# Attention on one Trainium2 core: the reciprocal of a slot's row sum moves behind the next slot's row maximum in VectorE's order

## The chip, the cores and the metric

The kernel runs on one core of a Trainium2 chip. The metric is the device time of one execution in microseconds, given as the median over several runs. A profiled execution gives the trace.

## The reference

Two layers on x of shape 8 x 512 x 256 with a context of the same shape: an mLSTM-like mixing with four heads and a GELU MLP (layer 0), then cross attention with 16 heads and a mixture of eight experts (layer 1). The change lies in the cross attention:

```
q = query @ W_Query + B_Query          # query: layer norm of x, 8 x 512 x 256
k = key @ W_Key + B_Key                # key = value = context
v = value @ W_Value + B_Value
q, k, v -> (B, L, H = 16, D = 64)
scores = einsum('bqhd,bkhd->bhqk', q, k) / D ** 0.5
probs = softmax(scores, axis=-1)
out = einsum('bhqk,bkhd->bqhd', probs, v)
return out.reshape(B, Lq, H * D) @ W_Output + B_Output
```

## The kernel before

`attention` goes through U = 64 units: eight batches times eight pairs of heads. A unit `u` is one pass of the outer loop; its NBL = 8 slots `j` are the two heads times four blocks of 128 query rows. Each engine has the two loops written out for itself, in an order of its own, and the engines meet by semaphores alone. Within its engine an instruction waits for the one in front of it, so the written order is the order of the work. The loop of each engine runs once more than there are units, so that the tail of unit u-1 lies in the first slots of unit u.

The way of a slot through the engines:

- TensorE, `score(u, j)` (L958): scores of 128 rows against 512 keys, two matmuls in float32r, into one of two PSUM banks (`S_BANK + j % 2`). It waits until the exponential of slot j-2 is done.
- VectorE, `row_max(u, j)` (L1153): the negated maximum of each row, into `nmax`. It waits for the scores (`s_ps`).
- ScalarE (L1093): the exponential with the maximum as bias, into `Pr`, with the row sum accumulated into `rsum`. It waits for `nmax` and for the turn of slot j-4.
- VectorE, `row_sum(u, j)` (L1158): the reciprocal of `rsum` into `rinv`. It waits for the exponential (`exp`).
- GpSimd (L1128): `Pr` times `rinv`. It waits for `rinv` and signals `pn`.
- TensorE, `turn(u, j)` (L969): four transposes of `Pr` into one of two banks. It waits for `pn` and for the copy of the turned slot j-2.
- VectorE, `keep(u, j)` (L1165), or ScalarE for slots 4 and 5 (L1112): the turned block into `PT`.

TensorE's order within a unit: in slot j `score(u, j)` and then `turn(u, j-2)` (in slots 0 and 1 it is turn 6 and turn 7 of the unit before). Besides, in slots 0 and 1 it projects the queries and keys of the next unit (`project`, L937), in slot 2 it weighs the values of the unit before (`weigh_values`, L979), in slot 4 it projects the values of the next (`project_values`, L946), in slots 5 and 6 it multiplies by the output weights (`output`, L989). In fourteen units it also turns rows (`turn_rows`, L999) or maps gates (`map_gates`, L1008), in slots 3 and 7.

VectorE's order within slot j: the reciprocal of slot j-1, the maximum of slot j, the copy of turned slot j-2. Besides, it takes part in the next unit's queries (L1140, slot 1) and keys (L1147, slot 2), in the layer norm for the experts in some units, and at slot 7 it takes the reciprocal of slot 7 and adds the outputs of the unit before to x (L1172).

The `% 4` of `Pr`, `nmax`, `rsum` and `rinv` gives each of them four buffers.

Of the kernel before, what the change touches and what calls it, by code (L numbers as in the profile page):

```python
# [826 lines left out]
def attention(nc, c, x_all, xnT_all, ctxT_all, first, Wq, Wk, Wv, Wo, gate_w, lg, rows, rows_in, out, landed):  # L827
# [3 lines left out]
    with ExitStack() as ctx:  # L831
# [33 lines left out]
        def there(u):  # L865
            return 0 <= u < U

        def routed(u, r):

            return u // HP - 1 if u >= HP and u % HP == r else None  # L870
# [16 lines left out]
        with nc.Block() as block:  # L887
# [247 lines left out]
            def _(dve):  # L1135
                def queries(u):
                    dve.wait_ge(s["qh"], u + 1)
                    for h in range(2):
                        own, other = slice(AD * h, AD * h + AD), slice(AD - AD * h, 2 * AD - AD * h)
                        ins = dve.scalar_tensor_tensor(out=q2[other, u % 2, h, :], in0=ps[own, A_BANK, :],  # L1140
                                                       scalar=b_s[own, 0, u % HP:u % HP + 1],
                                                       in1=q2[own, u % 2, h, :], op0=ALU.add, op1=ALU.subtract)
                    ins.then_inc(s["ql"], 1)

                def keys(u):
                    dve.wait_ge(s["kh"], u + 1)
                    dve.scalar_tensor_tensor(out=k_own[:, 1, :], in0=ps[:, A_BANK + 1, :],  # L1147
                                             scalar=b_s[:, 1, u % HP:u % HP + 1],
                                             in1=k_own[:, 0, :], op0=ALU.add, op1=ALU.subtract).then_inc(s["kl"], 1)

                def row_max(u, j):
                    dve.wait_ge(s["s_ps"], NBL * u + j + 1)
                    dve.tensor_reduce(nmax[:, j % 4:j % 4 + 1], ps[:, S_BANK + j % 2, :], AX.X, ALU.max, negate=True  # L1153
                                      ).then_inc(s["nmax"], 1)

                def row_sum(u, j):
                    dve.wait_ge(s["exp"], NBL * u + j + 1)
                    dve.reciprocal(rinv[:, j % 4:j % 4 + 1], rsum[:, j % 4:j % 4 + 1]).then_inc(s["rinv"], 1)  # L1158

                def keep(u, j):  # L1160
                    if j in ON_ACT:
                        return
                    dve.wait_ge(s["t_ps"], NBL * u + j + 1)
                    q = P * (j % TPB)
                    dve.tensor_copy(PT[:, u % 2, j // TPB, :, q:q + P],  # L1165
                                    ps[:, T_BANK + j % 2, :].rearrange("p (t q) -> p t q", t=TPB)).then_inc(s["pt_v"], 1)

                def add_out(u, half):
                    dve.wait_ge(s["y_ps"], 2 * u + half + 1)
                    at = (u // HP) * TPB + 2 * half  # L1170
                    xv = x_all[:, at:at + 2, :].rearrange("p t d -> p (t d)")
                    dve.tensor_tensor(xv, ps[:, Y_BANK - half, :], xv, ALU.add).then_inc(s["x"], 1)  # L1172

                def take_stats(b, t):
                    if t == 0:
                        dve.wait_ge(s["x"], 2 * HP * (b + 1))
                    ins = dve.bn_stats(stats[:, t, :], x_tile(b, t))
                    if t == TPB - 1:
                        ins.then_inc(s["stats"], 1)

                def finish_stats(b):
                    wait_apart(dve, s["stats"], b + 1)
                    for t in range(TPB):
                        ins = dve.bn_aggr(mv[:, t, :], stats[:, t, :])
                    ins.then_inc(s["mv"], 1)
                    dve.wait_ge(s["mv"], b + 1)
                    wait_count(dve, s["rstd"], b)
                    dve.tensor_scalar(ve[:, :], mv[:, :, 1], LN_EPS, None, ALU.add).then_inc(s["ve"], 1)

                def apply(b, t):  # L1190
                    if t == 0:
                        dve.wait_ge(s["rstd"], b + 1)
                    ins = dve.tensor_scalar(xn_tile(b, t), x_tile(b, t), mv[:, t, 0:1], rstd[:, t:t + 1],
                                            ALU.subtract, ALU.mult)
                    if t == TPB - 1:
                        ins.then_inc(s["xn"], 1)
# [11 lines left out]
                for u in range(U + 1):  # L1208
                    for j in range(NBL):
                        if there(u):  # L1210
                            if j >= 1:
                                row_sum(u, j - 1)
                            row_max(u, j)
                            if j >= 2:
                                keep(u, j - 2)
                        if j < 2 and there(u - 1):
                            keep(u - 1, NBL - 2 + j)
                        if there(u + 1):
                            if j == 1:
                                queries(u + 1)  # L1220
                            if j == 2:
                                keys(u + 1)
                        if 2 <= j < 2 + TPB and routed(u, NORM) is not None:
                            take_stats(routed(u, NORM), j - 2)
                        if j == 2 + TPB and routed(u, NORM) is not None:
                            finish_stats(routed(u, NORM))
                        if 2 <= j < 2 + TPB and routed(u, APPLY) is not None:
                            apply(routed(u, APPLY), j - 2)
                        if j == 7:
                            if there(u):  # L1230
                                row_sum(u, j)
                            if there(u - 1):
                                if u > 1:
                                    dve.wait_ge(s["x"], 2 * (u - 1))
                                add_out(u - 1, 0)
                                add_out(u - 1, 1)
# [503 lines left out]
```

## Time and profile before

| what | value |
|---|---|
| time, median of 3 runs | 1844.12 us (1844.11 to 1846.59) |
| the profiled execution's span | 1843.2 us |
| its mean granted TensorE clock | 0.947 |
| TensorE busy | 1663.1 us (90%) |
| VectorE busy | 1209.8 us (66%) |
| ScalarE busy | 843.8 us (46%) |
| GpSimd busy | 608.1 us (33%) |

The span reaches from the first to the last instruction of one profiled execution. The engines' shares are means over stages with different limits: the attention takes the stretch from about 370 to 1640 us, and the router and the experts follow it. TensorE's matmuls are pipelined, and the ends of their records are modelled. A granted clock of 1 is 2.4 GHz.

### The profile page before, as it was taken

To read this page: it belongs to the slowest core of one execution; us is meant where nothing else is said; L and a number is where in the kernel's file an instruction comes from. 1 tells how busy PE (TensorE), PEld (TensorE's weight loads), DVE (VectorE), ACT (ScalarE), POOL (GpSimd) and SP (SyncE) were. 2 spreads that over 40 slices of the span, in tenths; PEclk is the share of its full clock that TensorE was granted. 3 is DMA by queue.
4 is the path that set the end of the run, shared out by engine and by line. 5 is a ranking of instruction groups with operands and counts; after the bars stand their busy time and mean duration, and the time that the engine had idled before them with its cause. 6 is when DMAs were issued, how large, how long until landed. Compare 5 with 4: busy or idle time off the path is not lost. (4 is left out here: it accounts for less than half of the span.)

```text
span 1843.2 us, 25796 instructions
## 1 busy us (share of the span) xinstructions
PE 1663.1 (90%) x8789; PEld 1128.1 (61%) x8789; DVE 1209.8 (66%) x2689; ACT 843.8 (46%) x1870; POOL 608.1 (33%) x730
## 2 busy tenths in 40 slices
PE   6569999996999999999999999999999999973584
PEld 4447777754666666666666666666666766642352
DVE  6445656532777777776776776776777677757761
ACT  3324343431555555555555555555555555531110
POOL 2143445430333323332332332333232323220375
PEclk9669999997999999999999999999999999985697
DMA  8100000003323232323232322222223223213254
GB/s 254 27 23 12 12 12 1 1 0 106 69 47 69 47 92 46 69 69 69 47 92 47 67 72 61 54 65 74 56 60 79 59 53 86 46 45 99 44 85 58
DMA packets 68961, 109.46 MB, mean 59 GB/s; under 512 B 18400, under 2 KB 50400, under 8 KB 68832
## 3 DMA queue, kind: packets, MB, share of 16 engines
q1 hardware_dynamic: 62688, 99.29, 22.1%
q0 software_dynamic: 6144, 8.52, 3.0%
q8 instruction: 72, 1.18, 0.3%
q14 instruction: 57, 0.47, 0.1%
HBM read 27.84 MB, written 12.85 MB: 22 GB/s over the span
## 5 line engine op out<-in xcount | busy, mean ns | idle before, releaser
L1128 POOL TENSOR_SCALAR at_Pr<-at_Pr,at_rinv 128x512 f32<-128x512 f32 x512 | 355.8, 695 | 841.2 <-DVE at_rinv L1158 841.2
L1093 ACT ACTIVATE at_Pr<-at_ps,at_nmax 128x512 f32<-128x512 f32 x512 | 352.2, 688 | 535.2 <-DVE at_nmax L1153 533.6
L1153 DVE TENSOR_REDUCE at_nmax<-at_ps 128x1 f32<-128x512 f32 x512 | 351.2, 686 | 154.0 <-PE at_ps L958 142.5
L958 PE MATMUL at_ps<-at_k,at_q 128*128 128x512 f32 x1024 | 420.7, 492 | 10.8 <-DMA at_k<-at_k_own 9.1
L969 PE MATMUL at_ps<-k_ident,at_Pr 128*128 128x128 f32 x2048 | 309.8, 274 | 4.5 <-POOL at_Pr L1128 4.5
L969 PEld LDWEIGHTS at_ps<-k_ident,at_Pr 128*128 128x128 f32 x2048 | 250.5, 140 | 90.2 <-POOL at_Pr L1128 27.7
L1165 DVE COPY at_PT<-at_ps 128x512 f32<-128x512 f32 x384 | 261.4, 681 | 0.0
L958 PEld LDWEIGHTS at_ps<-at_k,at_q 128*128 128x128 f32 x1024 | 174.6, 191 | 130.7 <-issue 121.2
L979 PE MATMUL at_ps<-at_PT,at_V 128*64 128x512 f32 x1024 | 235.4, 602 | 0.9 <-DVE at_PT L1165 0.9
L1158 DVE RECIPROCAL at_rinv<-at_rsum 128x1 f32<-128x1 f32 x512 | 83.3, 163 | 161.1 <-ACT at_Pr L1093 159.1
L979 PEld LDWEIGHTS at_ps<-at_PT,at_V 128*64 128x64 f32 x1024 | 68.1, 137 | 122.5 <-issue 121.4
L989 PE MATMUL at_ps<-at_wo,at_oT 128*128 128x256 f32 x512 | 131.6, 380 | 0.8 <-ACT at_oT L1070 0.8
L459 PE MATMUL mm_ps<-mx_w,mm_hT 128*128 128x256 f32 x512 | 119.6, 382 | 0.0
L449 PE MATMUL mm_ps<-m_xnT,mx_w 128*128 128x512 f32 x256 | 112.6, 598 | 1.3 <-ACT m_xnT L598 1.3
L937 PE MATMUL at_ps<-m_ctxT,at_w_rest 128*128 128x512 f32 x224 | 105.9, 595 | 4.0 <-ACT m_xnT L1075 4.0
L946 PE MATMUL at_ps<-at_w_rest,m_ctxT 128*128 128x128 f32 x896 | 109.2, 275 | 0.0
L937 PE MATMUL at_ps<-m_xnT,at_w_rest 128*128 128x512 f32 x224 | 107.1, 601 | 0.0
L946 PEld LDWEIGHTS at_ps<-at_w_rest,m_ctxT 128*128 128x128 f32 x896 | 104.5, 192 | 0.0
L459 PEld LDWEIGHTS mm_ps<-mx_w,mm_hT 128*128 128x128 f32 x512 | 94.3, 190 | 16.1 <-issue 3.8
L1140 DVE SCALAR_TENSOR_TENSOR at_q<-at_ps,m_b_all,at_q 64x512 fp32r<-64x512 f32 x128 | 96.0, 750 | 11.0 <-ACT at_q L1053 8.2
L1093 ACT ACTIVATION_READ_ACCUMULATOR at_Pr<-at_ps,at_nmax 128x1 f32 x512 | 98.5, 192 | 0.0
L989 PEld LDWEIGHTS at_ps<-at_wo,at_oT 128*128 128x128 f32 x512 | 87.4, 190 | 8.3 <-ACT at_oT L1070 1.7
(236 smaller groups left out, 1996.5 us busy)
## 6 DMA issues: line engine op xcount, KB each, us to landing
at_k<-at_k_own SPq DMA_DIRECT2D x256, 256.0 KB, 4.3
k_x<-in_x SPq DMA_DIRECT2D x8, 512.0 KB, 8.5
mg_ctx<-in_ctx SPq DMA_DIRECT2D x8, 512.0 KB, 8.7
mx_ctxn<-in_ctx SPq DMA_DIRECT2D x8, 512.0 KB, 3.8
rows<-m_ctxT SPq DMA_DIRECT2D x16, 256.0 KB, 2.6
out<-k_x SPq DMA_DIRECT2D x8, 512.0 KB, 3.5
r_w<-in_L_ffn_w SPq DMA_DIRECT2D x16, 256.0 KB, 5.5
mx_w<-in_L_ffn_w SPq DMA_DIRECT2D x2, 1024.0 KB, 10.0
```

The lines of the kernel that those rows point to most:

```text
L449: ins = pe.matmul(ps[:, H_BANK + f % 4, :], w1_s[:, k, P * f:P * f + P], xnT_all[:, k, b * S:b * S + S], start=k == 0, stop=k == DC - 1)
L459: ins = pe.matmul(ps[:, Y_BANK + t // 2, D * (t % 2):D * (t % 2) + D], hT[:, f, P * t:P * t + P], w2_s[:, f, :], start=f == 0, stop=f == F ...
L937: ins = pe.matmul(ps[:, A_BANK + k, :], weights(k, d, hp), src[:, d, b * S:b * S + S], start=d == 0, stop=d == DC - 1)
L946: ins = pe.matmul(ps[:, A_BANK, P * t:P * t + P], ctxT_all[:, d, b * S + P * t:b * S + P * t + P], weights(2, d, hp), start=d == 0, stop=d ...
L958: ins = pe.matmul(ps[:, S_BANK + j % 2, :], q2[:, u % 2, h, q:q + P], k2[:, u % 2, h, part, :], start=part == 0, stop=part == 1)
L969: ins = pe.transpose(ps[:, T_BANK + j % 2, P * t:P * t + P], Pr[:, j % 4, P * t:P * t + P], c["ident"][:, :])
L979: ins = pe.matmul(ps[AD * h:AD * h + AD, O_BANK, :], V[:, u % 2, t, AD * h:AD * h + AD], PT[:, u % 2, h, t, :], start=t == 0, stop=t == TP ...
L989: ins = pe.matmul(ps[:, Y_BANK - half, D * (t % 2):D * (t % 2) + D], oT[:, P * t:P * t + P], wo_s[:, u % HP, :], start=True, stop=True)
L1093: act.activation(Pr[:, j % 4, :], ps[:, S_BANK + j % 2, :], ACT.Exp, bias=nmax[:, j % 4:j % 4 + 1], accum_out=rsum[:, j % 4:j % 4 + 1]).th ...
L1128: pool.tensor_scalar(Pr[:, n % 4, :], Pr[:, n % 4, :], rinv[:, n % 4:n % 4 + 1], 1.0, ALU.mult, ALU.mult).then_inc(s["pn"], 1)
L1153: dve.tensor_reduce(nmax[:, j % 4:j % 4 + 1], ps[:, S_BANK + j % 2, :], AX.X, ALU.max, negate=True).then_inc(s["nmax"], 1)
L1165: dve.tensor_copy(PT[:, u % 2, j // TPB, :, q:q + P], ps[:, T_BANK + j % 2, :].rearrange("p (t q) -> p t q", t=TPB)).then_inc(s["pt_v"], 1)
```

## The change

In VectorE's loop over the slots `row_max(u, j)` is issued first, and `row_sum(u, j - 1)` after it. Nothing else differs; the other engines' programs are the same.

```
                 for u in range(U + 1):
                     for j in range(NBL):
                         if there(u):
+                            row_max(u, j)
                             if j >= 1:
                                 row_sum(u, j - 1)
-                            row_max(u, j)
                             if j >= 2:
                                 keep(u, j - 2)
```

## Rows read from the trace of the kernel before

**Rows 1.** The page's part 1, busy time, share and instructions of each engine.
```profile
PE 1663.1 (90%) x8789; PEld 1128.1 (61%) x8789; DVE 1209.8 (66%) x2689; ACT 843.8 (46%) x1870; POOL 608.1 (33%) x730
```

**Rows 2.** Busy time of each engine by stretch, granted clock, DMA share.
```profile
370.00:1640.00 1270.00, 1241.32 (x6505) 825.22 (x6503) 895.10 (x1878) 670.49 (x1518) 383.90 (x533) 0.99 0.27 63
700.00:900.00 200.00, 199.42 (x1071) 132.94 (x1070) 146.83 (x305) 109.02 (x250) 61.45 (x88) 1.00 0.28 64
100.00:200.00 100.00, 89.70 (x441) 66.53 (x442) 47.57 (x114) 34.69 (x76) 42.37 (x39) 0.87 0.05 15
1620.00:1640.00 20.00, 16.14 (x83) 9.64 (x82) 12.78 (x29) 9.93 (x25) 6.91 (x10) 1.00 0.00 0
```

**Rows 3.** Who waited for whom, 500 to 1600 us: total, times, longest.
```profile
POOL at_Pr L1128 <- DVE at_rinv L1158: 763.4, 475, 3.2
ACT at_Pr L1093 <- DVE at_nmax L1153: 491.3, 416, 3.5
...
PEld at_ps L969 <- POOL at_Pr L1128: 18.7, 45, 0.7
```

**Rows 4.** Timeline of TensorE, one unit: start, length, what, count.
```profile
885.15 3.65 PE L979 MATMUL at_ps<-at_PT,at_V 128*64 128x512 f32 x16
888.73 0.74 PE L958 MATMUL at_ps<-at_k,at_q 128*128 128x512 f32 x2
...
890.21 0.60 PE L969 MATMUL at_ps<-k_ident,at_Pr 128*128 128x128 f32 x4
890.65 1.95 PE L946 MATMUL at_ps<-m_w_first,m_ctxT 128*128 128x128 f32 x16
892.36 0.71 PE L958 MATMUL at_ps<-at_k,at_q 128*128 128x512 f32 x2
...
894.02 0.82 PE L958 MATMUL at_ps<-at_k,at_q 128*128 128x512 f32 x2
894.67 0.60 PE L969 MATMUL at_ps<-k_ident,at_Pr 128*128 128x128 f32 x4
...
895.79 0.82 PE L958 MATMUL at_ps<-at_k,at_q 128*128 128x512 f32 x2
896.45 0.60 PE L969 MATMUL at_ps<-k_ident,at_Pr 128*128 128x128 f32 x4
...
897.49 0.66 PE L969 MATMUL at_ps<-k_ident,at_Pr 128*128 128x128 f32 x4
897.99 1.88 PE L937 MATMUL at_ps<-m_xnT,at_w_rest 128*128 128x512 f32 x4
...
903.32 1.08 PE L979 MATMUL at_ps<-at_PT,at_V 128*64 128x512 f32 x4
```

**Rows 5.** Timeline of VectorE, the same stretch.
```profile
887.82 0.15 DVE L1158 RECIPROCAL at_rinv<-at_rsum 128x1 f32<-128x1 f32 x1
889.51 0.69 DVE L1153 TENSOR_REDUCE at_nmax<-at_ps 128x1 f32<-128x512 f32 x1 [1.53 <-PE at_ps L958]
890.12 0.68 DVE L1165 COPY at_PT<-at_ps 128x512 f32<-128x512 f32 x1
...
896.41 0.16 DVE L1158 RECIPROCAL at_rinv<-at_rsum 128x1 f32<-128x1 f32 x1 [0.84 <-ACT at_Pr L1093]
896.65 0.69 DVE L1153 TENSOR_REDUCE at_nmax<-at_ps 128x1 f32<-128x512 f32 x1
```

**Rows 6.** Timeline of GpSimd, the same stretch.
```profile
896.74 0.69 POOL L1128 TENSOR_SCALAR at_Pr<-at_Pr,at_rinv 128x512 f32<-128x512 f32 x1 [1.08 <-DVE at_rinv L1158]
```

**Rows 7.** Timeline of TensorE, unit 11, which also turns rows.
```profile
664.63 0.74 PE L958 MATMUL at_ps<-at_k,at_q 128*128 128x512 f32 x2
...
666.55 0.60 PE L969 MATMUL at_ps<-k_ident,at_Pr 128*128 128x128 f32 x4
```

**Rows 8.** Timeline of TensorE, unit 12, which also maps gates.
```profile
684.29 0.74 PE L958 MATMUL at_ps<-at_k,at_q 128*128 128x512 f32 x2
...
686.66 0.60 PE L969 MATMUL at_ps<-k_ident,at_Pr 128*128 128x128 f32 x4
```

More of the change, by code:

```diff
@@ L1210, in _ @@
                         if there(u):
+                            row_max(u, j)
                             if j >= 1:
                                 row_sum(u, j - 1)
-                            row_max(u, j)
                             if j >= 2:
```

## The prediction

> **What bounds the kernel now.** I read the page first: TensorE is busy for 1663.1 of 1843.2 us, VectorE for 1209.8 [rows 1]. Then the busy time by stretch: the attention, roughly 370 to 1640 us, is 69% of the span; in 700 to 900 us TensorE is busy for 199.42 of 200 us at a granted clock of 1.00 [rows 2]. The reader is to see that what counts is only what makes TensorE wait. Next, who waits for whom: GpSimd waits 763.4 us for the reciprocal and ScalarE 491.3 us for the row maximum, but these idle times cost nothing; what TensorE's weight load pays for a missing GpSimd result is 18.7 us in 45 waits [rows 3]. So VectorE's order may give back at most some 20 us, and it can take as much as it likes.
>
> Last, the timeline. I call a pass of `for u` a unit and a pass of `for j` a slot. A unit takes 18.17 us (the weighing of the values starts at 885.15 and at 903.32) [rows 4], and there are 64 of them. In slot j TensorE does score(j), then turn(j-2), then extras; turn(j-2) needs reciprocal j-2 and GpSimd's scaling with it.
>
> **What the change does to a dependence.** Nothing is added or removed: 448 of the 512 reciprocals (slots 0 to 6 of each unit) move behind the next slot's maximum. Before, reciprocal j-1 waits only for its exponential. After, it is queued behind row_max(j), and VectorE holds it while row_max(j) waits for score(j). A score that is late on TensorE now makes the reciprocal of the slot before late, with it GpSimd's multiplication, and with that turn(j-1), which stands in TensorE's order right behind score(j+1). A loop arises that runs from TensorE through VectorE and GpSimd back to TensorE. The ScalarE side gains (the exponential no longer waits for the reciprocal before it), but that takes nothing off TensorE, which hardly waits for it.
>
> **The length of the new loop**, from the end of score(j) to the first matmul of turn(j-1):
> - end of score to start of the maximum: 0.04 us (888.73 + 0.74 = 889.47; the maximum starts at 889.51) [rows 4, 5].
> - start of the maximum to start of the reciprocal: no row of before shows this pair without a wait. The nearest is maximum to copy, 889.51 to 890.12, 0.61 us [rows 5]. I take 0.61, since VectorE starts that copy before the maximum's 0.69 us record ends. If the next one starts only at the record's end, it is 0.69.
> - start of the reciprocal to start of GpSimd's scaling: 896.41 to 896.74, 0.33 us; the scaling lasts 0.69 [rows 5, 6].
> - its end to TensorE: 896.74 + 0.69 = 897.43; the turn starts at 897.49, so 0.06 [rows 4, 6].
>
> The sum is 0.04 + 0.61 + 0.33 + 0.69 + 0.06 = 1.73 us; with 0.69 it is 1.81.
>
> The skill bears on the second item. The Trainium skill, VectorE: DVE Perf Modes, section "The DRAIN you can't avoid", says that the next VectorE operation does not start until the pipe has emptied; read as the record's end that gives 1.81 and the larger sum below. The copy's row shows a start 0.08 us ahead of that end, so the trace does not agree with this reading, and the main sum is without it.
>
> **The room that TensorE leaves**, from the end of score(j) to the first matmul of turn(j-1), as it is now [rows 4]:
> - j = 3 (turn 2): 889.47 to 890.21, 0.74 us: only turn(1) and score(4) lie between, because the long weighing (3.65 us) stands ahead of score(3). Until now reciprocal 2 was done during that weighing, at 887.82 [rows 5]. Missing: 1.73 - 0.74 = 0.99.
> - j = 5 (turn 4): 892.36 + 0.71 = 893.07 to 894.67, 1.60. Missing: 0.13.
> - j = 6 (turn 5): 894.02 + 0.82 = 894.84 to 896.45, 1.61. The 0.13 by which turn(4) is late lies inside and makes it 1.74. Missing: nothing.
> - j = 7 (turn 6): 895.79 + 0.82 = 896.61 to 897.49, 0.88; this turn is already stalled by GpSimd (0.88 is the length of today's wait, with today's reciprocal at 896.41). Missing: 0.85.
> - j = 1, 2, 4: a projection (1.88), the weighing (3.65) or the projection of the values (1.95) lies between, with a turn or a score on top, so the room is longer than the loop. Nothing.
> - Reciprocal 7 is in no other place than before, behind its own exponential.
>
> A turn that has stalled costs 0.06 more (897.49 to 897.99 is 0.50; the same distance is 0.44 for the unstalled turn 2, 890.21 to 890.65 [rows 4]); that counts for turns 2 and 4. A plain unit thus loses 1.05 + 0.19 + 0.85 = 2.09 us.
>
> What else the shift reaches: at the unit's boundary the next maximum stands behind the addition of the outputs, as before; its exponential and reciprocal come no later than TensorE's own shift of 0.85 us. The weighing waits for the copy of turned slot 7, which stands a projection and a score ahead of it. The keys' transfer, which SyncE issues behind VectorE's part of the keys in slot 2, is not wanted before the next unit's first score. I count nothing for these.
>
> Fourteen units are not plain, those that also turn rows or map gates (routed units, u of at least 8, u % 8 of 3 or 4): TensorE has more to do between, and the room at j = 3 is 664.63 + 0.74 = 665.37 to 666.55, 1.18 us, in the seven with row turns [rows 7], and 684.29 + 0.74 = 685.03 to 686.66, 1.63 us, in the seven with gates [rows 8]; the extra stands in slot 7 again, so I take the same rooms there. They lose (0.55 + 0.06) + 0.19 + 0.55 = 1.35, and 0.16 + 0.19 + 0.10 = 0.45 us.
>
> **The sum.** 50 x 2.09 + 7 x 1.35 + 7 x 0.45 = 104.5 + 9.5 + 3.2 = 117 us. The profiled execution's span is 1843.2 us, 0.9 below the median 1844.12 of the runs, and the shift is added to the median: 1961 us. With 1.81 in place of 1.73 the misses are 1.07, 0.21, 0.93: 2.33 a plain unit, 1.6 and 0.7 in the others, 132 us in all, 1976. If the late first matmuls cost less than they seem, because TensorE's queue recovers the 0.06 and the 0.13, what remains is 0.99 + 0.85 = 1.84, and 1.1 and 0.1 in the others: 100 us, 1944. So this case runs from 1940 to 1995.
>
> **The rivals.**
> - *Faster.* The moved maximum lets the exponentials start sooner, and the only regular stall of TensorE, that of turn 6, goes. Its price is at most the 18.7 us of waits in 1100 us (60 units) [rows 3], for 64 units some 20 us: 1824. It decides if reciprocal 6 comes before 896.41, but it now stands behind the maximum that starts at 896.65 [rows 5]. Only a score 7 that ends earlier than TensorE's saturated order allows would do it. Chance 0.03.
> - *Nothing.* The order does not reach TensorE, 1844 within 3.7 us (0.2%, which is about what a measurement of this kernel tells from no change). It needs a loop no longer than 0.74 us, while GpSimd's scaling alone lasts 0.69. Chance 0.04.
> - *One stall swallows the other.* The shift from turn 2 leaves the rest of the unit looser, and only one of the two large terms is paid: 50 x 1.05 + 7 x 0.6 or so, 57 us, about 1901; range 1850 to 1940. Against it: both rooms are measured from a score that the first stall shifts too. Chance 0.08.
> - *Clock or cascade.* TensorE will be busy for about 17.9 of 20.3 us (18.17 less today's 0.3 of waits, and 18.17 + 2.09). In 100 to 200 us it was busy for 89.70 of 100 at a mean granted clock of 0.87, while in 1620 to 1640, with 16.14 of 20 busy in short waits, it was 1.00 [rows 2]. If the attention got 0.87, those 17.9 us would take 2.7 us more a unit: another 171 us, about 2130. The Trainium skill, TensorE: Matmul & The Clock Gate, section "What's actually happening", has the clock depend on how busy TensorE has been, which speaks for this rival; the trace agrees that it falls in places, and not in 1620 to 1640. Short of that, a second wait that I priced at nothing (a late copy of a turned block, an exponential behind ScalarE's copy) may add half a microsecond a unit, 1995 to 2030. Chance together 0.10.
>
> The forecast has 0.75. Faster 0.03, same 0.04, slower 0.93. The range that leaves out no more than 2 in 10 is 1930 to 2005; the likeliest case's own is 1940 to 1995.
>
> **What the new profile would show.** The unit is about 20.3 us long, with waits of turns 2 and 6 for GpSimd (about 1.0 and 1.2 us of idle TensorE each unit) and a small one of turn 4; the total of that wait grows from 18.7 us to over 100. ScalarE's wait for the maximum becomes shorter per unit relative to its work, GpSimd still waits for the reciprocal. VectorE shows the reciprocal 0.6 us behind the start of each maximum. The granted clock stays at 1.00. I would be wrong if the reciprocal follows the maximum much sooner, if TensorE's waits do not show behind slots 3 and 7, or if the clock falls.

## The result and the profile after

The changed kernel takes 1953.78 us (1953.43 to 1955.21, four runs), the kernel before 1844.11 in the same session. The ratio is 1.0594 (95% interval 1.0579 to 1.0609): 109.7 us slower, where 117 were forecast (1961), inside the range. The profiled execution's span is 1953.5 us.

Busy time by stretch (start and length, then TensorE, its weight load, VectorE, ScalarE, GpSimd, the granted clock, DMA), against [rows 2]:

```profile
700.00:900.00 200.00, 188.51 (x992) 120.87 (x991) 132.98 (x280) 101.58 (x232) 55.09 (x80) 1.00 0.26 59
100.00:200.00 100.00, 89.70 (x423) 65.72 (x423) 45.51 (x112) 34.81 (x76) 38.79 (x37) 0.83 0.05 14
1730.00:1750.00 20.00, 15.98 (x74) 8.82 (x74) 11.47 (x27) 8.26 (x22) 6.24 (x10) 0.91 0.00 0
```

In 700 to 900 us TensorE was busy for 199.42 us, now for 188.51, at the same clock of 1.00. It waits, and its work runs no slower. The other two rows are read in the section on the prediction. Who waits for whom between 500 and 1600 us, against [rows 3]:

```profile
POOL at_Pr L1128 <- DVE at_rinv L1158: 795.6, 434, 3.8
ACT at_Pr L1093 <- DVE at_nmax L1153: 525.9, 344, 3.7
DVE at_nmax L1153 <- PE at_ps L958: 302.5, 265, 2.3
PEld at_ps L969 <- POOL at_Pr L1128: 150.7, 215, 1.5
...
DVE at_rinv L1158 <- ACT at_Pr L1093: 41.9, 54, 0.8
```

Read the fourth row first: the turn's weight load waits 150.7 us for GpSimd's scaled block where it waited 18.7. (Stalled matmuls have 72.8 us on TensorE's own row as well; the two overlap and are not to be added.) The last row is the other side. VectorE's reciprocal now waits for its exponential in 54 places, about one in each unit, that of slot 7, since in the other slots the exponential is long done when the reciprocal is reached. ScalarE's wait for the maximum, which the new order might seem to shorten, is 525.9 us in fewer units, about 9.6 us a unit of 20.16 us where it was 8.1 a unit of 18.17: it waits for TensorE at one remove.

One unit on TensorE, against [rows 4]. The weighing starts at 947.85 and at 968.01, so the unit is 20.16 us long where it was 18.17:

```profile
947.85 3.65 PE L979 MATMUL at_ps<-at_PT,at_V 128*64 128x512 f32 x16
951.43 0.73 PE L958 MATMUL at_ps<-at_k,at_q 128*128 128x512 f32 x2
952.00 0.60 PE L969 MATMUL at_ps<-k_ident,at_Pr 128*128 128x128 f32 x4
952.35 0.71 PE L958 MATMUL at_ps<-at_k,at_q 128*128 128x512 f32 x2
953.87 0.66 PE L969 MATMUL at_ps<-k_ident,at_Pr 128*128 128x128 f32 x4 [0.80 <-POOL at_Pr L1128]
954.36 1.95 PE L946 MATMUL at_ps<-at_w_rest,m_ctxT 128*128 128x128 f32 x16
956.06 0.71 PE L958 MATMUL at_ps<-at_k,at_q 128*128 128x512 f32 x2
...
957.72 0.81 PE L958 MATMUL at_ps<-at_k,at_q 128*128 128x512 f32 x2
958.49 0.66 PE L969 MATMUL at_ps<-k_ident,at_Pr 128*128 128x128 f32 x4
...
959.66 0.82 PE L958 MATMUL at_ps<-at_k,at_q 128*128 128x512 f32 x2
960.32 0.60 PE L969 MATMUL at_ps<-k_ident,at_Pr 128*128 128x128 f32 x4
960.67 0.71 PE L958 MATMUL at_ps<-at_k,at_q 128*128 128x512 f32 x2
962.19 0.66 PE L969 MATMUL at_ps<-k_ident,at_Pr 128*128 128x128 f32 x4 [0.81 <-POOL at_Pr L1128]
962.68 1.88 PE L937 MATMUL at_ps<-m_xnT,at_w_rest 128*128 128x512 f32 x4
...
968.01 1.51 PE L979 MATMUL at_ps<-at_PT,at_V 128*64 128x512 f32 x6
```

VectorE and GpSimd around turns 2 and 6 of this unit, against [rows 5, 6]:

```profile
952.20 0.69 DVE L1153 TENSOR_REDUCE at_nmax<-at_ps 128x1 f32<-128x512 f32 x1 [2.24 <-PE at_ps L958]
952.80 0.15 DVE L1158 RECIPROCAL at_rinv<-at_rsum 128x1 f32<-128x1 f32 x1
...
960.52 0.69 DVE L1153 TENSOR_REDUCE at_nmax<-at_ps 128x1 f32<-128x512 f32 x1 [1.18 <-PE at_ps L958]
961.12 0.15 DVE L1158 RECIPROCAL at_rinv<-at_rsum 128x1 f32<-128x1 f32 x1
```

```profile
953.12 0.69 POOL L1128 TENSOR_SCALAR at_Pr<-at_Pr,at_rinv 128x512 f32<-128x512 f32 x1 [3.55 <-DVE at_rinv L1158]
...
961.44 0.69 POOL L1128 TENSOR_SCALAR at_Pr<-at_Pr,at_rinv 128x512 f32<-128x512 f32 x1 [1.25 <-DVE at_rinv L1158]
```

The loop is read along one chain. Score 3 starts at 951.43 and ends at 952.16 (0.04 us ahead of the maximum at 952.20); the reciprocal starts 0.60 later at 952.80, GpSimd 0.32 later at 953.12 for 0.69, and turn 2 at 953.87, 0.06 behind its end: 1.71 us in all. The same chain of slot 7 runs from 959.66 + 0.82 = 960.48 over 960.52, 961.12 and 961.44 to 962.19, again 1.71.

The rooms of before (the time that TensorE leaves from the end of a score to the turn that hangs on it) are now all as long as the loop. From the end of score 3 to turn 2 it is 1.71 us (0.74 before); from the end of score 5, 956.06 + 0.71 = 956.77, to turn 4 at 958.49 it is 1.72 (1.60); from the end of score 7 to turn 6 it is 1.71 (0.88). That is 0.97 + 0.12 + 0.83. Turns 2 and 4, now stalled, have 0.49 to the next work where it was 0.44, 0.05 each. The sum is 2.02 us, and the unit grew by 1.99.

### The profile page after: what moved, and what is told of

Its sections match the earlier page's. It is cut to its first block and busy times, and to the rows that moved or that the text cites. A ratio compares the mean times of both kernels' runs of the same rounds, so it can differ in the third digit from the quotient of the medians.

```text
span 1953.5 us, 25796 instructions
## 1 busy us (share of the span) xinstructions
PE 1692.2 (87%) x8789; PEld 1114.4 (57%) x8789; DVE 1197.4 (61%) x2689; ACT 845.1 (43%) x1870; POOL 606.6 (31%) x730
## 5 line engine op out<-in xcount | busy, mean ns | idle before, releaser
L969 PE MATMUL at_ps<-k_ident,at_Pr 128*128 128x128 f32 x2048 | 317.9, 278 | 89.4 <-POOL at_Pr L1128 89.0
L969 PEld LDWEIGHTS at_ps<-k_ident,at_Pr 128*128 128x128 f32 x2048 | 235.0, 140 | 217.6 <-POOL at_Pr L1128 183.7
```

The costliest lines, as they stand in the source:

```text
L969: ins = pe.transpose(ps[:, T_BANK + j % 2, P * t:P * t + P], Pr[:, j % 4, P * t:P * t + P], c["ident"][:, :])
```

## The experiments

Eight kernels ran. "Before" in a session is the kernel before on the same chip: 1845.42 us for the first four, 1844.18 for the last four. The changed kernel was not run again beside them; where a run is compared with it, its 1953.78 us stands, whose own before was 1844.11. "A unit grew" means the time from one unit's first score to the next unit's, read from the profiled executions.

### The maximum first in slot 3 alone

```
                             if j in (3,):
                                 row_max(u, j)
                             if j >= 1:
                                 row_sum(u, j - 1)
                             if j not in (3,):
                                 row_max(u, j)
```

> The maximum goes first in slot 3 alone; in all other slots the reciprocal stays first. My theory (a loop of 1.71 us from the end of a score through maximum, reciprocal and GpSimd to the turn, against the room that TensorE leaves): turn 2 is late by 1.71 - 0.74 = 0.97 us, with 0.05 for the stalled start 1.02 a plain unit, 0.5 and 0.1 in the routed ones: +55 us, 1900 (1893 to 1907); turn 6 waits as in the kernel before. Rival 'one stall swallows the other': alone this one pays the same, but then the run with slot 7 alone and this one together exceed the whole change by 40 us or more. Rival 'the whole order matters' (cascade over the slots): alone it costs under 30 us, below 1875.

Measured: 1901.1 us (1898.76 to 1902.9), ratio 1.0303 (1.0288 to 1.0319): +55.7 us, where +55 were expected. TensorE's timeline:

```profile
931.16 0.71 PE L958 MATMUL at_ps<-at_k,at_q 128*128 128x512 f32 x2
932.68 0.66 PE L969 MATMUL at_ps<-k_ident,at_Pr 128*128 128x128 f32 x4 [0.81 <-POOL at_Pr L1128]
...
939.31 0.71 PE L958 MATMUL at_ps<-at_k,at_q 128*128 128x512 f32 x2
940.00 0.66 PE L969 MATMUL at_ps<-k_ident,at_Pr 128*128 128x128 f32 x4
```

Turn 2 stands 1.52 us behind the start of the score ahead of it, as in the changed kernel; turn 6 stands 0.69 behind its own, as before. A plain unit grew by 1.0 us. The stall is made by this one slot's order and stays in its place.

### The maximum first in slot 7 alone

The same edit with `(7,)` in place of `(3,)`.

> The maximum goes first in slot 7 alone. Theory: turn 6 is late by 1.71 - 0.88 = 0.83 us beyond its wait of today, 0.5 and 0.1 in the routed units: +46 us, 1890 (1883 to 1897); turn 2 has no wait. With e1_only_slot3 the two make 101 of the 110 us of the change. Rival 'swallow': the sum of both is far above 110. Rival 'cascade': under 25 us.

Measured: 1882.74 us (1882.01 to 1883.35), ratio 1.0203 (1.0187 to 1.0219): +37.3 us, 9 less than expected and just outside the stated range. Now it is the other way about:

```profile
941.56 0.71 PE L958 MATMUL at_ps<-at_k,at_q 128*128 128x512 f32 x2
942.11 0.60 PE L969 MATMUL at_ps<-k_ident,at_Pr 128*128 128x128 f32 x4
...
948.70 0.72 PE L958 MATMUL at_ps<-at_k,at_q 128*128 128x512 f32 x2
950.22 0.66 PE L969 MATMUL at_ps<-k_ident,at_Pr 128*128 128x128 f32 x4 [0.80 <-POOL at_Pr L1128]
```

In a plain unit the price is as expected: 1.52 us from score to turn 6 where it was 0.68. What is less is the routed units. Before, TensorE waited 4.0 us in 7 places, 0.6 us in each, for ScalarE's copy of the turned rows (L1075), one projection further on. This wait is not in the profile of this run, nor in that of the changed kernel; with turn 6 on time again (the projection moved, below) it is back, 3.4 us in 6 places. So in seven units a part of the shift is taken out of another wait; a pair of routed units pays 0.15 us for turn 6 and not 0.6, some 3 of the missing 9 us. Of the rest, 1.5 us is that the first two units, still filling, pay 0.1 together. What remains is about what this profiled execution was shorter outside the regular units: 1.5 us ahead of the attention's first score, and 1.6 us in the very last weighing, which took 3.65 us at a granted clock of 1.00 where the kernel before took 5.24 at 0.71.

With slot 3 alone the sum is 93 us of 109.7, and turn 4, 0.17 in each unit, would bring another 11: 104. The last 6 us are not divided by a run (the changed kernel's profile has some 5 us more than the one before in places outside its regular units, see the section on the prediction). Neither of the two large terms is swallowed by the other, and there is no cascade that needs all slots.

### The maximum first in slots 1, 2 and 4

The same edit with `(1, 2, 4)`.

> The maximum goes first in slots 1, 2 and 4, where TensorE has long work (a projection, the weighing, the projection of values) before the turn that needs the moved reciprocal. Theory: the room is over 2.4 us, the loop 1.71 to 2.15, so no change: 1844 within 4 us. Rival 'the earlier exponentials bring something of their own': 1835 or less. Rival 'each moved reciprocal costs': 3/7 of the change, 1890.

Measured: 1846.28 us (1844.94 to 1849.54, eleven runs), ratio 1.0004 (0.9995 to 1.0013). TensorE's wait for GpSimd, 500 to 1600 us, is 18.9 us where it was 18.7:

```profile
PEld at_ps L969 <- POOL at_Pr L1128: 18.9, 46, 0.7
```

Three of the seven moved reciprocals cost nothing that these runs can tell (at most 2.4 us by the interval). Nor do the earlier exponentials bring anything. That the place of TensorE's long work decides what a moved reciprocal costs fits this; the runs below that move this work show it.

### The maximum first in slots 1, 2, 4, 5 and 6

The same edit with `(1, 2, 4, 5, 6)`.

> The maximum goes first in slots 1, 2, 4, 5 and 6; in slots 3 and 7 the reciprocal stays first. Theory: only turn 4 is late, by 0.11 plus 0.05 for its stalled start, 0.16 us in each of 64 units: +10 us, 1854 (1848 to 1860). Rival 'each moved reciprocal costs': 5/7 of the change, 1922. Rival 'small misses are absorbed by TensorE's queue': 1844.

Measured: 1849.58 us (1847.27 to 1850.67, eleven runs), ratio 1.0022 (1.0013 to 1.0031): +4.2 us, where +10 were expected (inside the stated range). Both sides of the difference can be read:

```profile
931.35 0.82 PE L958 MATMUL at_ps<-at_k,at_q 128*128 128x512 f32 x2
932.12 0.66 PE L969 MATMUL at_ps<-k_ident,at_Pr 128*128 128x128 f32 x4
...
934.30 0.71 PE L958 MATMUL at_ps<-at_k,at_q 128*128 128x512 f32 x2
934.85 0.62 PE L969 MATMUL at_ps<-k_ident,at_Pr 128*128 128x128 f32 x4
```

Turn 4 is late as in the changed kernel (0.77 us behind score 6, with 0.49 to the next work). But turn 6 stands 0.55 us behind the score, not 0.68: it waits no more. The reason is not a faster exponential. With the reciprocal first in slot 7, turn 6 follows the end of score 6 over maximum, exponential, reciprocal and scaling by 2.65 us (894.84 to 897.49 in [rows 4]). Here score 6 ends at 931.35 + 0.82 = 932.17, and 2.65 later is 934.82, which is just when TensorE gets to turn 6 (934.85), because turn 4's delay lies between. So the 0.17 of turn 4 is taken out of the 0.13 and 0.05 that turn 6 waited anyway, and plain units cost nothing. A pair of routed units, where turn 6 did not wait before, grew by 0.33 us, 2.3 in all. The other 2 are in the last unit: its weighing took 4.98 us in place of 3.65, at a granted clock of 0.84 in 1624 to 1635 us. In miniature this is the rival in which one stall swallows the other. In the whole change it cannot happen, for there the wait of turn 6 counts from score 7, behind turn 4.

### The changed kernel with the projection ahead of turn 6

```
                         if j == 0 and there(u + 1):
                             project(u + 1, j)
                         if j < 2 and there(u - 1):
                             turn(u - 1, NBL - 2 + j)
                         if j == 1 and there(u + 1):
                             project(u + 1, j)
```

> The changed kernel, and in slot 0 TensorE projects the next unit's queries before it does turn 6, not after it. Theory: the projection fills the room behind score 7, so the wait of turn 6 goes: its start comes 0.55 us behind the score's, not 1.52, with 0.05 for the stalled start 1.02 us a plain unit less, 0.5 and 0.1 in the routed ones: -55 us against the changed kernel, 1899 (1890 to 1907). Rival: the wait is GpSimd's or the clock's and shows up at turn 7 or elsewhere in the unit; then within 15 us of 1954.

Measured: 1902.01 us (1901.57 to 1904.53), ratio 1.0319 to before (1.0303 to 1.0334), 52 us below the changed kernel, where 55 were expected. VectorE's order is the changed one; only TensorE has its long work in another place:

```profile
938.28 0.71 PE L958 MATMUL at_ps<-at_k,at_q 128*128 128x512 f32 x2
938.83 1.88 PE L937 MATMUL at_ps<-m_xnT,at_w_rest 128*128 128x512 f32 x4
940.55 0.60 PE L969 MATMUL at_ps<-k_ident,at_Pr 128*128 128x128 f32 x4
```

The projection starts 0.55 us behind the score and turn 6 follows it without a wait. The unit is 1.02 us shorter than in the changed kernel (19.14 us). Turn 2 still waits, as it should: its room was not touched.

### The kernel before with the same move

TensorE's loop as in the section above; VectorE's order is that of the kernel before.

> The kernel before with the same move of the projection ahead of turn 6, VectorE's order untouched. Theory: today's wait of turn 6 goes too: its start stands 0.68 us behind the score's start and would stand 0.55 behind, with 0.05 for the stalled start 0.18 a unit: -10 us, 1834 (1830 to 1839). Rival: the pair behind it (maximum of slot 0, copy of turn 6) is late and a new wait takes its place: 1844 or more.

Measured: 1834.54 us (1833.88 to 1836.11), ratio 0.9949 (0.9935 to 0.9962): 9.6 us faster than the kernel before, where 10 were expected.

```profile
929.96 0.72 PE L958 MATMUL at_ps<-at_k,at_q 128*128 128x512 f32 x2
930.52 1.88 PE L937 MATMUL at_ps<-m_xnT,at_w_rest 128*128 128x512 f32 x4
932.23 0.60 PE L969 MATMUL at_ps<-k_ident,at_Pr 128*128 128x128 f32 x4
```

The unit is 17.97 us long (929.96 to 947.93 from score 0 to score 0) and TensorE's waits for GpSimd are gone from the list. This is the fastest version found, and it needs the old order in VectorE.

### The changed kernel with the weighing in slot 3

```
-                        if j == 2 and there(u - 1):
+                        if j == 3 and there(u - 1):
                             weigh_values(u - 1)
```

> The changed kernel, with the weighing of the values moved from slot 2 to slot 3, behind turn 1. Theory: it now fills the room of turn 2 (1.02 us a unit gained) and leaves that of turn 1, which keeps some 1.1 us between the end of score 2 and its start; the loop is 1.71 plus 0.35 that maximum 2 waits behind VectorE's queries plus 0.1 for the reciprocal behind them, 2.15, so turn 1 waits some 1.1 to 1.2: 1960 (1948 to 1970). Rival: what was missing is long work anywhere before slot 4, and turn 1 has room: 1899.

Measured: 1987.74 us (1987.4 to 1989.0), ratio 1.078 (1.0764 to 1.0797): 34 us above the changed kernel, where 6 were expected. The sign tells the theories apart (the rival had it at 1899), the size was outside my range. TensorE and VectorE:

```profile
956.39 1.03 PE L958 MATMUL at_ps<-at_k,at_q 128*128 128x512 f32 x2
...
957.61 0.72 PE L958 MATMUL at_ps<-at_k,at_q 128*128 128x512 f32 x2
957.76 0.69 DVE L1153 TENSOR_REDUCE at_nmax<-at_ps 128x1 f32<-128x512 f32 x1
958.48 0.16 DVE L1158 RECIPROCAL at_rinv<-at_rsum 128x1 f32<-128x1 f32 x1
...
959.56 0.66 PE L969 MATMUL at_ps<-k_ident,at_Pr 128*128 128x128 f32 x4 [1.23 <-POOL at_Pr L1128]
```

The loop was right: score 2 ends at 956.39 + 1.03 = 957.42, the maximum starts 0.34 later behind the queries, the reciprocal 0.72 after it, and turn 1 at 959.56: 2.14 us, where 2.15 were expected. My room was wrong. I had put it at 1.1 us. An unstalled turn stands 0.57 behind its score's start, so it is 957.61 + 0.57 - 957.42 = 0.76. Turn 1 therefore loses 2.14 - 0.76 + 0.05 = 1.43 a unit and 1.02 are gained at turn 2: 0.41 in a plain unit. The profile has 0.44, some 21 us in 48 plain units. The rest is the routed units. There turn 2 had little to give back, about 0.1 and 0.6, because the extra work of slot 3 had widened its room, while turn 1 pays its 1.43 in full: a pair takes 2.1 us more than in the changed kernel, seven of them 15 us. (Together that is 36; this profile was 3 us shorter ahead of the attention.) The expectation had left this out too.

### The changed kernel with half of GpSimd's scaling

```
-                    pool.tensor_scalar(Pr[:, n % 4, :], Pr[:, n % 4, :], rinv[:, n % 4:n % 4 + 1], 1.0,
+                    pool.tensor_scalar(Pr[:, n % 4, 0:S // 2], Pr[:, n % 4, 0:S // 2], rinv[:, n % 4:n % 4 + 1], 1.0,
```

> The changed kernel, but GpSimd scales only the first 256 of the 512 columns of each block, so the other half of the probabilities stays unnormalised: work left out. Theory: GpSimd's 0.69 us are a part of the loop; at about 0.36 the loop is 1.38, turn 2 waits 0.64 and turn 6 0.50 beyond today's, turn 4 nothing: 63 us above the kernel before in place of 110, 1907 (1897 to 1917). Rival: the loop closes over ScalarE or VectorE alone, GpSimd is beside it: 1954.

This kernel leaves the second half of each block unscaled. Measured: 1915.64 us (1913.54 to 1918.26), ratio 1.0388 (1.0372 to 1.0404): 38 us below the changed kernel, where 47 were expected. The groups of instructions give the reason for the difference (busy time and mean of one, then the idle time before):

```profile
L1128 POOL TENSOR_SCALAR at_Pr<-at_Pr,at_rinv 128x256 f32<-128x256 f32 x489 | 234.4, 479 | 958.9 <-DVE at_rinv L1158 958.9
```

Half of the columns takes 0.479 us, not my guess of 0.36. So the loop should be 1.71 - 0.21 = 1.50, and TensorE shows it, from the end of score 3 to turn 2 (936.79 to 938.28, 1.49):

```profile
936.05 0.74 PE L958 MATMUL at_ps<-at_k,at_q 128*128 128x512 f32 x2
...
938.28 0.66 PE L969 MATMUL at_ps<-k_ident,at_Pr 128*128 128x128 f32 x4 [0.59 <-POOL at_Pr L1128]
```

Turn 2 then misses 0.76 and turn 6 0.62, with 0.05 for the start 1.43 a plain unit; in the profile it grew by 1.41. That 50 times 1.43 is just the 71.5 us that this kernel takes more than before is chance: a routed pair adds 0.4, seven of them 3 us, and the last unit adds nothing. The unit is 0.60 us shorter than in the changed kernel: 0.21 each at turns 2 and 6, and the 0.17 of turn 4, whose room of 1.60 the shorter loop no longer fills. So GpSimd's time is in the loop one for one.

## Why the prediction was right

- **What bounds.** That only TensorE's waits count held: VectorE's wait for scores grew to 302.5 us and ScalarE's for the maximum to 9.6 us a unit, and the sum comes out without a price for either. One sign was read the wrong way round: ScalarE's wait was to become shorter per unit.
- **The loop.** Forecast 1.73 us from four rows of before, measured 1.71. The pair that before did not show, maximum to reciprocal, is 0.60 to 0.61, as its nearest row, the copy; the reading with 0.69 falls. With it falls the larger sum, and with it the reading of the Trainium skill's "The DRAIN you can't avoid" (VectorE: DVE Perf Modes) by the record's end: the reciprocal starts 0.09 us ahead of it. That section adds, which I had left out, that an instruction that is not held starts earlier; so it is here.
- **The rooms.** Turn 2: 0.99 forecast, 0.97 measured. Turn 4: 0.13 and 0.12. Turn 6: 0.85 and 0.83. Turn 5: late by nothing beyond its share of turn 4's. The cost of a stalled start, 0.06, was 0.05. The idle of about 1.0 and 1.2 us that was to show ahead of turns 2 and 6 is 0.8 each on the matmuls' row and 1.24 each on the weight load's. Together 2.09 forecast and 1.99 measured a plain unit; over 48 of them that is 5 us of the miss. (The sum for the low end has a slip: without turn 4 a unit with gates still misses 0.10 twice, 0.2 and not 0.1, 0.7 us in all.)
- **Slots 1, 2 and 4 at nothing.** Held (1.0004 alone).
- **The first two units** were counted as plain, 4.2 us together. From the first score of unit 0 to that of unit 2 it was 35.38 us before and is 36.67 now: 1.3 us, 3 us of the miss. Why the pipeline pays less while it fills was not looked into.
- **The routed units** are the other term that was mis-sized. I gave a pair of them 1.35 + 0.45 = 1.80 us and had not asked whether TensorE waits for something else there. It did, for ScalarE's row copy, 0.6 us once in each pair, and a late turn 6 runs into this wait. Between the two profiled executions the three units around such a pair grew by 3.2 us, so the pair by 1.2; seven pairs make 4 us of the miss.
- **The rivals.** "One stall swallows the other" is refuted for the two large stalls by the runs with one slot each. It holds on a small scale only, for turn 4 with the old order in slot 7. "Nothing" falls. "Faster" falls: exponentials that start sooner bring nothing where tried alone (slots 1, 2 and 4), and the stall of turn 6 goes by TensorE's order, not by VectorE's. The cascade fails with the runs that move one slot or a few. The clock was 1.00 in every stretch read from 470 to 1730 us. Only in the last unit, where the row of 1730 to 1750 us has 0.91, did it fall. The weighing there, whose matmuls are the same, took 5.35 us where the kernel before took 3.65, so that rival was worth 1.7 us. Before:

```profile
1626.71 3.65 PE L979 MATMUL at_ps<-at_PT,at_V 128*64 128x512 f32 x16
```

After, behind waits of 0.81, 1.09 and 0.58 us within 5 us:

```profile
1734.88 5.35 PE L979 MATMUL at_ps<-at_PT,at_V 128*64 128x512 f32 x16
```

Whether the new order brings this fall is open: the runs with slot 3 or slot 7 alone show it in neither of their last two weighings.

- **How much of the agreement is luck.** With the three corrections the sum is 117 - 5 - 4 - 3 = 105 us. From the first score to the end of the last weighing the attention took 1191.2 us before and 1298.2 after, 107.0 more, and 1.7 of them are the clock: that part closes. The other 3.3 of the 110.3 us between the two profiled spans lie ahead of the attention (its first score starts at 458.99 us, before at 455.66), in code that is the same, with a clock of 0.83 in 100 to 200 us against 0.87. So the forecast missed by more than the two totals show: 5 us that it had not priced hid a part of the miss. The medians contain such differences too, so no sum is exact to the microsecond.

## What to carry to other kernels

On an engine that works in its written order, as VectorE does here, moving an instruction ahead of another one gives the second all waits of the first. Before such a swap, take the length of the new loop (the wait's release through every engine back to the one that bounds) and compare it at each place with what the bounding engine has to do in between; where long work lies between, the swap is free (slots 1, 2 and 4 here), and where it does not, the difference is the price, and it can be added up place by place. Ask at each place, too, whether the bounding engine has another wait close behind: that one takes up a part of the price, as in the routed units. The same list of rooms shows where the bounding engine's long work should stand: ahead of the instruction whose input comes late.

## What the runs showed of the hardware

- A 128 x 256 scaling on GpSimd takes 0.479 us and a 128 x 512 one 0.692: half of the columns saves 31%. If the time is a fixed part and one that goes with the columns, the fixed part is about 0.27 us, an estimate from these two sizes.
- On VectorE the reciprocal starts 0.60 us behind the start of a 0.69 us maximum, but 0.72 behind maximum 2, which follows the queries: the 0.72 of 957.76 to 958.48 (the run with the weighing in slot 3) is seen in 63 of the 64 units there and in the changed kernel. The last unit, which has no queries of a next one, has 0.60. The Trainium skill, VectorE: DVE Perf Modes, section "Two Vector instructions with no wait between them", has a rule under which an instruction is held until the earlier ones have finished, if its input starts in another group of 32 partitions than the first input from the same memory of the last instruction that read it. The queries' second instruction reads SBUF from partition 64 on, the maximum reads only PSUM, and the reciprocal reads SBUF from partition 0: by that rule it is held here and in no other slot. The trace agrees (0.72 is behind the 0.69 us of the maximum, 0.60 is ahead of it, and the hold goes with the queries), and no run here tried it by itself.
- A turn that has stalled has 0.49 to 0.50 us to the next work, one that has not 0.43 to 0.44, so each new stall costs 0.05 us beyond its wait.
- In the changed kernel's 700 to 900 us TensorE was busy for 188.51 of 200 us, with two waits of 0.8 us in each unit, and the granted clock stayed at 1.00; with the weighing in slot 3 it was busy for 182.21 us in the same stretch, with waits of 1.23 and 0.8 us a unit, also at 1.00.
